# Other instruction orders and other PSUM banks in a four-layer graph network kernel, with stages and waits kept

## The reference

```python
# per graph: x [128,256], adj [128,128]
x = ln(x + (adj @ (x @ W0 + b0)) / adj.sum(-1))                    # layer 0
qk = x @ Wqk; q, k = split(qk); v = x @ Wv                         # layer 1
w = (q * (adj @ k)).sum(-1) / 16 ; x = ln(x + softmax(w)[:, None] * v)
s = (q @ k.T) * scale * (adj + adj)   # 8 heads of 32              # layer 2
x = ln(x + (softmax(s) @ v) @ Wo.T + bo)
h = relu(hypergraph_conv(x, adj, W1, b1)); h = layer_norm(h, gamma, beta)
x = ln(x + hypergraph_conv(h, adj, W2, b2) + x)                    # layer 3
```

## Time and profile before

| what | before |
|---|---|
| median of 3 runs | 1855.54 us (1854.58 to 1856.67) |
| the profiled execution | 1856.53 us |
| its span | 1854.8 us |
| instructions in the span | 52832 |
| granted clock of PE, mean | 0.992 |

### The profile page before, as it was taken

How to read it: one execution, slowest core, us unless ns; L and a number is a source line. 1 busy time by engine, 2 the same in 40 slices (tenths; PEclk the granted TensorE clock), 3 DMA queues, 4 the chain that set the end, 5 groups by cost and what they waited for, 6 DMA issues and landing times.

```text
span 1854.8 us, 52832 instructions
## 1 busy us (share of the span) xinstructions
PE 1809.7 (98%) x15357; PEld 1589.4 (86%) x15357; DVE 1446.6 (78%) x3909; ACT 1444.9 (78%) x4463; POOL 1439.4 (78%) x2857
## 2 busy tenths in 40 slices
...
GB/s 130 7 41 41 17 23 40 40 40 40 6 34 40 40 40 35 5 40 40 40 40 27 12 40 40 40 40 16 24 40 40 40 40 5 35 40 40 37 20 12
DMA packets 95434, 62.94 MB, mean 34 GB/s; under 512 B 10288, under 2 KB 94768, under 8 KB 95408
## 3 DMA queue, kind: packets, MB, share of 16 engines
...
...
## 4 chain that ended last, share of the span: by engine, by line
PE 94%; DVE 2%; issue 1%; POOL 1%; ACT 1%; SPq 0%; DMA 0%; DVEq 0%; POOLq 0%
PE ps L437 55%; PE ps L540 6%; PE ps L508 6%; PE ps L500 5%; PE ps L516 4%; PE ps L422 4%; PE ps L453 3%; PE ps L529 3%; PE ps L490 2%; PE ps L474 2%; PE ps L447 2%; DVE z L975 1%; PE ps L427 1%; SPq L390 0%; DMA x<-in_L_gnn_Wq_dram 0%
## 5 line engine op out<-in xcount | busy, mean ns | idle before, releaser
L673 ACT ACTIVATE z<-z,z_max 128x128 f32<-128x128 f32 x1024 | 399.1, 400 | 0.1
L763 POOL TENSOR_TENSOR ln_rs<-ln_ve,minus_half 128x1 f32<-128x1 f32 x640 | 351.8, 550 | 50.2
L783 POOL TENSOR_TENSOR z<-z,z_rcp 128x1024 f32<-128x1024 f32 x128 | 242.9, 1898 | 39.6 <-DVE z_rcp L993 39.6
L766 POOL TENSOR_SCALAR ln_nm<-ln_mv,ln_rs 128x1 f32<-128x1 f32 x640 | 169.3, 265 | 109.8 <-POOL ln_rs L763 109.8
L612 ACT ACTIVATE h<-h,ln_nm,ln_rs 128x512 f32<-128x512 f32 x128 | 104.5, 816 | 155.7 <-POOL ln_nm L766 154.3
L761 POOL TENSOR_TENSOR ln_ve<-ln_mv,eps_col 128x1 f32<-128x1 f32 x640 | 121.5, 190 | 116.6 <-DVE ln_mv L899 116.4
L437 PE MATMUL ps<-w1T,txT 128*128 128x512 f32 x768 | 210.1, 409 | 1.0 <-DVE txT L909 0.9
L975 DVE SCALAR_TENSOR_TENSOR z<-ps,a_hold 128x512 f32<-128x512 f32 x256 | 174.2, 681 | 41.5 <-PE ps L500 33.1
L437 PE MATMUL ps<-w2T,mnT 128*128 128x256 f32 x1536 | 206.0, 283 | 0.0
L673 ACT ACTIVATION_READ_ACCUMULATOR z<-z,z_max 128x1 f32 x1024 | 202.9, 198 | 0.0
L437 PEld LDWEIGHTS ps<-w2T,mnT 128*128 128x128 f32 x1536 | 192.5, 188 | 10.0 <-issue 2.0
...
## 6 DMA issues: line engine op xcount, KB each, us to landing
x_in<-in_x_dram SPq DMA_DIRECT2D x128, 128.0 KB, 2.2
a_hold<-in_adj_dram SPq DMA_DIRECT2D x128, 128.0 KB, 2.3
out_dram<-y_out SPq DMA_DIRECT2D x128, 128.0 KB, 1.9
a_in<-in_adj_dram SPq DMA_DIRECT2D x128, 64.0 KB, 1.9
...
```

Source lines behind the costliest of these rows:

```text
L673: m = act.activation(z[:, g % 2, h, :], z[:, g % 2, h, :], ACT.Exp, bias=z_max[:, g % 2, h:h + 1], accum_out=z_sum[:, g % 2, h:h + 1])
L763: pool.tensor_tensor(rs[n][:, g:g + 1], ve[n][:, g:g + 1], minus_half[:, :], ALU.pow).then_inc(root_made[n], 1)
L766: pool.tensor_scalar(nm[n][:, g:g + 1], mv[n][:, g, 0:1], rs[n][:, g:g + 1], -1.0, ALU.mult, ALU.mult).then_inc(shift_made[n], 1)
L783: pool.tensor_tensor(zg, zg, z_rcp[:, g % 2, :].unsqueeze(2).to_broadcast([P, HEADS, P]), ALU.mult)\
```

## The change

All the order lists are replaced, and with them the bank of nearly every product. The functions that build the stages are the same. Three moves go across the loop's edge: `mp.0`, `mp.1` (with `hT` and `hb` kept one group ahead) and `x2c.0`, `x2c.1` were done one iteration ahead and now belong to the iteration's own group. The first and last lines of the loop's lists:

```diff
 ORDER_TEXT = {
     "pe": """
-        at.0+:5 at.1+:3 v2.1:4 sc1.0:0 sc0.0:6 v2.2:2 at.2+:0 ax.0+:3 sc1.1:1 mp.2:5 at.3+:0 ax.1+:3 h0.0+:4
...
-        h1.3:7 x2t.0+:6 y.1:0 mn.2:3 x2t.1+:2 mp.0+:7 v2.0+:6 x2t.2+:5 x2t.3+:1 y.2:4 k0.0+:1 mn.3:4 mp.1+:3
-        q1.0+:2 k1.0+:6 y.3:0 q0.0+:6
+        at.0+:0 v2.1:4 at.1+:1 sc0.0:2 sc1.0:5 at.2+:7 ax.0+:0 mp.0:4 at.3+:1 ax.1+:4 sc1.1:2 sc0.1:6
+        h0.0+:1 ax.2+:3 mp.1:7 v2.2:6 ax.3+:7 h0.1+:4 h0.2+:3 pt.0:0 mp.2:5 sc0.2:3 mp.3:2 cx.0:0 x1t.0+:1
...
+        x2t.3+:1 y.3:5 q0.0+:1 k0.0+:7 k1.0+:0 q1.0+:3
     """,
     "act": """
-        v2.1 at.0+ at.1+ v2.2 at.2+ ax.0+ exp1.0 mp.2 at.3+ ax.1+ exp0.0 ax.2+ exp1.1 exp0.1 ax.3+ pt.0
...
+        v2.1 at.0+ at.1+ at.2+ ax.0+ mp.0 at.3+ exp0.0 exp1.0 ax.1+ mp.1 ax.2+ exp0.1 exp1.1 pt.0 ax.3+
...
     "pool": """
...
-        ln1_root.3+ x3b.2 x2c.0+ ln3_root.3 x2c.1+ ln4_root.0 ln4_root.1 ln4_root.2 x3b.3 ln4_root.3
...
+        ln3_root.0 wm.0+ ln2_root.3 c3.0 ln3_root.1 x3b.0 ln3_root.2 ln1_root.0+ ln3_root.3 ln1_root.1+
+        ln1_root.2+ x3b.1 ln1_root.3+ x3b.2 ln4_root.0 x3b.3 hT.0+ ln4_root.1 ln4_root.2 hb.0+ ln4_root.3
     """,
     "sp": """
-        lh.0+ la.0++ la.1++ store.0 la.2++ la.3++ lx.0++ lh.1+ lx.1++ store.1 lh.2+ lx.2++ lx.3++ store.2
-        lh.3+ store.3
+        la.0++ lh.0+ store.0 la.1++ la.2++ la.3++ lh.1+ lx.0++ lx.1++ lx.2++ store.1 lh.2+ store.2 lh.3+
+        store.3 lx.3++
     """,
```

More of the change, by code:

```diff
@@ L47 @@
-        h1.3:7 x2t.0+:6 y.1:0 mn.2:3 x2t.1+:2 mp.0+:7 v2.0+:6 x2t.2+:5 x2t.3+:1 y.2:4 k0.0+:1 mn.3:4 mp.1+:3
-        q1.0+:2 k1.0+:6 y.3:0 q0.0+:6
+        at.0+:0 v2.1:4 at.1+:1 sc0.0:2 sc1.0:5 at.2+:7 ax.0+:0 mp.0:4 at.3+:1 ax.1+:4 sc1.1:2 sc0.1:6
+        h0.0+:1 ax.2+:3 mp.1:7 v2.2:6 ax.3+:7 h0.1+:4 h0.2+:3 pt.0:0 mp.2:5 sc0.2:3 mp.3:2 cx.0:0 x1t.0+:1
+        sc1.2:6 pt.1:4 wo.0:1 sc1.3:2 sc0.3:6 cx.1:5 amx.0+:1 h0.3+:4 xg.0+:2 v2.3:6 x1t.1+:0 tx.0:3 wo.1:2
+        amx.1+:1 pt.2:4 h1.0:3 cx.2:4 amx.2+:5 x1t.2+:1 pt.3:2 wo.2:7 xg.1+:6 cx.3:0 x1t.3+:3 amx.3+:4
@@ L49 @@
+        tx.1:5 xg.2+:2 wo.3:1 xg.3+:6 tx.2:7 h1.1:4 wt.0+:5 h1.2:3 mn.0:0 tx.3:7 v1.0+:4 pb.0+:3 v1.1+:5
+        h1.3:6 v1.2+:2 v1.3+:4 mn.1:1 y.0:2 mn.2:7 x2t.0+:0 y.1:1 mn.3:5 v2.0+:2 x2t.1+:3 y.2:6 x2t.2+:4
+        x2t.3+:1 y.3:5 q0.0+:1 k0.0+:7 k1.0+:0 q1.0+:3
     """,
     "act": """
-        v2.1 at.0+ at.1+ v2.2 at.2+ ax.0+ exp1.0 mp.2 at.3+ ax.1+ exp0.0 ax.2+ exp1.1 exp0.1 ax.3+ pt.0
-        ln0_norm.0+ v2.3 mp.3 cx.0 ln0_norm.1+ exp0.2 x1t.0+ pt.1 exp1.2 amx.0+ ln2_norm.0 x1t.1+ cx.1
@@ new lines @@
+        ln0_norm.0+ v2.2 mp.2 cx.0 x1t.0+ mp.3 exp0.2 pt.1 exp1.2 cx.1 ln0_norm.1+ amx.0+ ln2_norm.0 exp1.3
+        tx.0 exp0.3 pt.2 ln0_norm.2+ x1t.1+ amx.1+ v2.3 cx.2 amx.2+ relu.0 x1t.2+ pt.3 ln0_norm.3+
+        ln2_norm.1 cx.3 x1t.3+ tx.1 amx.3+ ln2_norm.2 ln3_norm.0 tx.2 wexp.0+ ln2_norm.3 relu.1 tx.3 mn.0
+        relu.2 ln3_norm.1 relu.3 ln3_norm.2 mn.1 ln1_norm.0+ ln3_norm.3 mn.2 x2t.0+ ln1_norm.1+ ln1_norm.2+
+        mn.3 x2t.1+ ln1_norm.3+ x2t.2+ x2t.3+ ln4_norm.0 hbc.0+ ln4_norm.1 v2.0+ k0.0+ q0.0+ ln4_norm.2
@@ L58 @@
+        k1.0+ q1.0+ ln4_norm.3
     """,
     "dve": """
[L60 to L69, removed]
@@ L70 @@
[L70 removed]
+        asum.0+ z0.0 zmax0.0 z1.0 ax_lo.0+ zmax1.0 z1.1 z0.1 zmax0.1 zrcp.0 ax_lo.1+ ax_lo.2+ zmax1.1 h0.0+
+        ln0_stats.0+ h0.1+ ln0_aggr.0+ h0.2+ zrcp.1 ln0_stats.1+ ln0_stats.2+ z0.2 ax_lo.3+ ln0_aggr.1+
+        zmax0.2 cx_lo.0 ln0_aggr.2+ x1t_lo.0+ z1.2 drcp.0 zmax1.2 wo.0 ln2_stats.0 ln2_aggr.0 z1.3 z0.3
+        zrcp.2 zmax1.3 h0.3+ cx_lo.1 xg.0+ zmax0.3 ln0_stats.3+ tx_lo.0 ln0_aggr.3+ wo.1 zrcp.3 ln2_stats.1
+        h1.0 x1t_lo.1+ ln2_aggr.1 cx_lo.2 ln3_stats.0 wo.2 ln3_aggr.0 ln2_stats.2 ln2_aggr.2 xg.1+ x1t_lo.2+
@@ new lines @@
+        cx_lo.3 x1t_lo.3+ tx_lo.1 wo.3 xg.2+ ln2_stats.3 xg.3+ ln2_aggr.3 tx_lo.2 wmax.0+ h1.1 wnorm.0+ h1.2
+        ln3_stats.1 ln3_aggr.1 tx_lo.3 pcol.0+ v1.0+ ln3_stats.2 ln1_stats.0+ ln3_aggr.2 v1.1+ ln1_aggr.0+
+        h1.3 mn_lo.0 v1.2+ ln3_stats.3 ln1_stats.1+ ln3_aggr.3 ln1_aggr.1+ v1.3+ mn_lo.1 y.0 ln1_stats.2+
+        ln1_stats.3+ ln1_aggr.2+ ln1_aggr.3+ x2t_lo.0+ ln4_stats.0 mn_lo.2 mn_lo.3 ln4_aggr.0 y.1 x2t_lo.1+
+        y.2 ln4_stats.1 x2t_lo.2+ x2t_lo.3+ ln4_aggr.1 ln4_stats.2 ecnt.0+ y.3 ln4_aggr.2 ln4_stats.3
@@ L71 @@
+        ln4_aggr.3
     """,
     "pool": """
-        mask.0+ xb.0+ xb.1+ x2c.2 xb.2+ xb.3+ am.0+ probs.0 ln0_root.0+ ln0_root.1+ probs.1 dmax.0 hT.0+
-        ln2_root.0 ln0_root.2+ dinv.0 x2c.3 ln0_root.3+ probs.2 ln2_root.1 probs.3 wm.0+ c3.0 ln3_root.0
-        ln2_root.2 ln2_root.3 hb.0+ x3b.0 ln3_root.1 ln1_root.0+ ln1_root.1+ x3b.1 ln3_root.2 ln1_root.2+
-        ln1_root.3+ x3b.2 x2c.0+ ln3_root.3 x2c.1+ ln4_root.0 ln4_root.1 ln4_root.2 x3b.3 ln4_root.3
+        mask.0+ xb.0+ xb.1+ am.0+ x2c.0 x2c.1 xb.2+ probs.0 xb.3+ ln0_root.0+ probs.1 x2c.2 dmax.0
@@ L103 @@
     "pool": """
-        mask.0+ xb.0+ xb.1+ am.0+ xb.2+ xb.3+ ln0_root.0+ ln0_root.1+ ln0_root.2+ ln0_root.3+ hT.0+ wm.0+
-        hb.0+ ln1_root.0+ ln1_root.1+ ln1_root.2+ ln1_root.3+ x2c.0+ x2c.1+
+        mask.0+ xb.0+ xb.1+ xb.2+ hT.0+ am.0+ xb.3+ ln0_root.0+ ln0_root.1+ ln0_root.2+ ln0_root.3+ hb.0+
+        wm.0+ ln1_root.0+ ln1_root.1+ ln1_root.2+ ln1_root.3+
     """,
```

52 lines of the change are left out of this document (27 added, 25 removed).

## The result

The changed kernel takes **1864.09 us** (median of 5 runs, 1862.08 to 1865.89); the kernel before, run beside it, takes 1855.54 us (1854.58 to 1857.25). The ratio is 1.0045, with a 95% interval of 1.0031 to 1.006: a little slower, by more than the measurement's uncertainty. The forecast was 1866.5.

The account below looks back on a forecast made before the run. PE was taken as the bound: 53.6 us of stages plus 2.5 us of waits per iteration. Waits rising to 2.9 over 31 iterations add 11 us to 1854.8, giving 1866.5 at the median; range 1859.5 to 1880.

Parts of the forecast that it names:

- The loop's edge: At at.0, the loop's first product: PE waits 1.0 us for ACT's k1 read-out, behind POOL's chain to ln4_root.1.
- POOL's ten items: On POOL after ln3_root.3: five roots, three x3b and hT without idle, 10.06 us, so ln4_root.1 ends at T + 14.4.
- One sign: In the changed kernel's profile, POOL was to show no idle between ln3_root.3 and ln4_root.3.
- ax.1: Behind mp.0 on PE, same bank 4: a wait of 0.6 us for ACT's copy of mp.0.
- ax.2 and mp.1: On PE, needing banks of sc1.1 and sc0.1: waits for DVE's z stages, 0.2 + 0.15 us.
- cx.0, cx.1 and q0.0: On PE: waits of 0.3 and 0.4 us behind ACT's pt copies, and 0.15 us at q0.0 for x2t.3's read-out.
- PE's own work: PE's stages over one iteration: unchanged by the change, again 53.6 us, with five sc groups and eight exits.
- The sum: All waits of an iteration: 2.9 us against 2.5, so period 56.5 and +11 us in all; expected to err low.
- SP and outside the loop: SP's wait at store.0 is covered by about 4 us; lists outside the loop change 0, plus or minus 2 us.
- Faster: Rival, chance 0.35: ln4_root.1 ends by T + 13.4, at.0 waits for nothing, 1.9 us of waits, 1837 us.
- Much slower: Rival, chance 0.05: a further wait of 0.6 us an iteration, such as pt.0's behind POOL's queue, 1885 us.
- The view by weight loads: Whole loop, chance 0.01: weight loads bound PE, 7.1 us of each iteration could go, 1635 us.

Follow-up runs that it names:

- experiment 3: The changed kernel with hT moved early on POOL, from ahead of ln4_root.1 to behind ln3_root.0: 1834.48 us, ratio 0.9883.
- 6: The changed kernel with hT behind ln4_root.1 on POOL and ecnt.0 moved behind ln4_aggr.2 on DVE: 1847.91 us, ratio 0.9949.
- 5: The changed kernel with hT one place later on POOL, behind ln4_root.1: 1915.47 us, ratio 1.0312.

## Why the prediction was right

**The loop's edge: right from ln3_root.3 on; its start was set by something else.** POOL's ten items from ln3_root.3 to ln4_root.1 were to take 10.06 us; the two rows of POOL above are 952.03 and 962.11, or 10.08. h1.3 ends at T = 947.41, so ln3_root.3 ends at T + 4.6, not T + 4.3. I had it released by DVE's aggr, and that is not what holds it. These are the first rows of ln1_root.0 and ln3_root.3 on POOL, and DVE's two aggr, the first of which is the last one of ln3:

```profile
949.57 0.19 POOL L762 TENSOR_TENSOR ln_ve<-ln_mv,eps_col 128x1 f32<-128x1 f32 x1
...
950.78 0.19 POOL L762 TENSOR_TENSOR ln_ve<-ln_mv,eps_col 128x1 f32<-128x1 f32 x1
```

```profile
950.05 0.36 DVE L900 BATCH_NORM_AGGREGATE ln_mv<-ln_st 128x2 f32<-128x6 f32 x2
```

The aggr was there at T + 2.8, as forecast. POOL was still at ln1_root.0, and its timeline shows no wait for another engine from `wm` at 940.73, ahead of T, to the end of ln4_root.1. So the chain to at.0 is POOL's own queue, from before h1.3 on. From ln4_root.1 to k1's start 2.4 us were forecast (14.4 to 16.8) and 2.44 are there (962.11 to 964.55). k1 is read at T + 17.8 for 17.5. The products end 0.2 later than forecast too, so that 1.17 us of wait remain for the 1.0. One sign did not hold as written: POOL is idle once between ln3_root.3 and ln4_root.3, for 0.30 us ahead of ln4_root.2. ln4_root.2 ends at 963.66, before ACT is through with q0, so this does not reach k1.

**ax.1: right.** 0.66 for 0.6.

**ax.2 and mp.1: right in kind.** 0.07 and 0.15 for 0.35 together. Missed beside them was sc0.1, 0.26, the first that meets DVE's z row; so the three together have 0.48.

**cx.0, cx.1 and q0.0: too large.** cx.0 waits for nothing (0.3 forecast). cx.1's 0.15 (0.4 forecast) is no wait but the price of a cx group right behind sc, the same in experiments 3 and 6; q0.0 has 0.01 for 0.15. In their place x1t.0 has 0.35 (0.15 of it the exit from a cx group), because the norm of ln0 comes late, and x2t.3 has 0.17. I had counted x2t.3, cx.2 and cx.3 as 0.1 together.

**PE's own work: right within 0.1.** The transposes (at.2, x1t.0, pt.1, x1t.3) pay 0.15 for an exit where I had put 0.20 for all; the sum shrinks by 0.2, and cx.1 takes 0.15 of that back.

**The sum: right, with errors that cancel.** The forecast was 2.9 us of waits against 2.5, a period of 56.5; on the same count the trace has 2.8. The trace has 56.42 against 56.15: 31 x 0.27 = 8.4, the spans differ by 7.5 and the medians by 8.55. The two terms that I worked out by walking POOL and ACT held to 0.2; those read from slack around cx were twice or more too large, and by about as much as I had left out. That the two kinds of error met is luck, since the forecast rests on the small difference of two sums. The sum was expected to err low and erred high.

**SP and outside the loop: right.** No row of PE waits for a transfer at at.1. From the first at.0 of the second iteration to that of the last the kernels differ by 7.7 us; everything outside, the two other lists included, differs by 0.2 us the other way. So the difference lies in the loop's equal iterations.

**The rivals.** *Faster* did not come: ln4_root.1 ended 0.3 later. The rival's first way there, an earlier ln3 from DVE or ACT, would have brought nothing, since POOL was not waiting for it. Its condition, ln4_root.1 by T + 13.4, names a needed link but not a sufficient one: it ends at T + 12.9 in experiment 3, where at.0 waits for nothing and the time is 1834 (the rival's price was 1837), and at T + 12.8 in 5 and 6, where at.0 waits all the same and the times are 1915 and 1848. *Much slower* did not come: pt.0 has no wait. The view by weight loads (the Trainium skill, Perfetto Trace Analysis, section Identifying the Most-Contended Engine, as quoted in the prediction) gave 14% of room. The trace of experiment 3 has 48.95 us of loads in a period of 55.50, 88%, and none of the twelve orders and edits has a median below 1833; no run here shows that figure right or wrong as a bound.

**What the prediction did not see.** A list of waits is not a list of gains. Each excess has its value only while the one behind it is covered: of at.0's 1.17 us the bank alone returned 0.26, and the order on ACT 0.26; removing the cause on POOL returned 0.93 (56.42 to 55.49). ax.1's 0.66 returned nothing at all. So the time of the changed kernel was predicted by the right wait, and the answer to "what would mend it" only came from following that wait back to the item on POOL. Still open is which of the late rows (mp.1's copy, z, the norm of ln0) one would have to move together to gain more than experiment 3.
